# The shared expert's last two groups moved behind the routed rows

## The chip, the cores and the metric

The kernel runs on one core of one Trainium2 chip. The metric is the device time of one execution in microseconds (us). The core has five engines that run their own queues in order and meet at semaphores: PE (TensorE, matrix products into the PSUM banks), ACT (ScalarE), DVE (VectorE), POOL (GpSimd) and SP (SyncE, which issues DMA transfers). POOL issues DMA transfers too, among them scatters to rows named by an index, with or without an addition to what lies there.

## The reference, cut to what matters

Two transformer-like layers over 32 x 256 tokens of 128 features. The change works in the last part of the second layer. Its input `x` is normalised to `xn`, and `xn` once more, with learned weights, to `a`:

```
rh          = gelu(a @ res_inter_w + res_inter_b)          # the shared expert: every token
res_mlp_out = rh @ res_output_w + res_output_b
h           = gelu(dispatched @ inter_w[e] + inter_b[e])   # the routed experts: 8 of them, 1024 rows each
expert_out  = h @ output_w[e] + output_b[e]
moe_out     = each token's own expert row, times its gate
coef        = softmax(a @ res_coef)
out         = res_mlp_out * coef[:, :1] + moe_out * coef[:, 1:] + xn
final       = x + conv_part(xn) + out     # conv_part: long convolution, gated projection, normalisation
```

So the output of a token is a sum of the stream (`x + xn`), the convolution part, the shared expert and the routed expert.

## The kernel before, in words

The 8192 tokens are 64 tiles of 128, in 16 groups of four (`GROUPS = 16`, `GROUP = 4`). The function `shared_and_last` holds the whole last stage. Work of one group of 512 tokens on an expert is two steps on PE: `make_hidden` (`L1523`, four products of 512 columns, 128 hidden units each; on ACT `activate`, `L1695`, applies gelu) and `make_out` for the shared expert (`L1533`) or `make_tiles` for the routed ones (`L1550`), 16 products each. In float32 one product shows as two matmul rows.

The expert sequence counts `ALL = 32` groups: 0 to 15 are the shared expert over the tokens in order, 16 to 31 the routed rows, two groups for each of eight experts. A helper `half(i)` on each engine takes the steps in turn: odd `i` is a `make_hidden`, even `i` the output step of the group before. Halves 0 to 11 run beside the convolution. From half 12 they run in the loop over the gated projection, one in each round `g` and two in round 8.

A round `g` of that loop: PE turns four tiles (`turn_y`, `L1584`), takes its half, and projects (`project`, `L1592`). ACT applies gelu (`L1709`), the gate's tanh (`gate`, `L1714`) for group `g - 1`, its half, and normalises group `g - 2` (`normalise`, `L1723`). DVE scales group `g - 3` (`scale`, `L1914`), multiplies with the gate and measures group `g - 1` (`gate_and_measure`, `L1895` to `L1904`), takes its half (`evict`, `L1845` and `L1850`, which adds the shared expert's weighted output to the stream), forms an offset (`make_offset`, `L1909`) and adds the projection's bias (`add_bias`, `L1887`). POOL takes the root of group `g - 1` (`root`, `L1422`), adds the normalised group `g - 3` to the stream (`add`, `L1429`) and scatters three token tiles to their experts' rows in DRAM (`L1035`), until all 64 are out. `add(g)` waits for `scaled` and for `evicted`, so a finished group of the stream has all but its routed part. SP then stores it to the output (`store`, `L1371`).

After the loop come the routed rows. SP loads each group of rows (`load_rows`, `L1376`), PE turns it (`turn_rows`, `L1561`), DVE takes it (`take_rows`, `L1867` to `L1870`), PE and ACT make the hidden layer and the four tiles, DVE adds the bias and weighs the tile (`put_y`, `L1879` and `L1881`), and POOL scatters it with an addition to the output rows (`L1473`), one scatter for each of the 64 tiles, after a wait for all stores (`stored`). POOL ends with a wait for every scatter. The weights of experts 0 to 6 are loaded by `load_pack` (`L1380`) as soon as the last `turn_y` is done, since they lie where the projection's input lay. Those of expert 7 would lie over the shared expert's weights, so their load waits for the last shared `make_out`.

Of the kernel before, what the change touches and what calls it, by code (L numbers as in the profile page):

```python
# [17 lines left out]
ALU = mybir.AluOpType  # L18
# [3 lines left out]
P = 128  # L22
B, T, D = 32, 256, 128
# [1246 lines left out]
def shared_and_last(nc, a, m, out):  # L1270
# [16 lines left out]
    ALL = 2 * GROUPS  # L1287
    PER = GROUPS // E
    with ExitStack() as ctx:
        def sb(name, shape, dt=F32):  # L1290
# [54 lines left out]
                "y_turned", "yT_ready", "projected", "biased", "tanh", "gated", "stats", "raised", "rstd", "offset",  # L1345
                "normal", "scaled", "added", "scattered", "tile_downed", "tile_summed", "tile_ready")))
        tiles = lambda g: slice(g * GROUP, g * GROUP + GROUP)

        @block.sync
        def _(sp):  # L1350
# [28 lines left out]
            def load_pack(e):  # L1379
                sp.dma_start(m["packs"][:, e, :], a["experts1"][:, e, :]).then_inc(sem[f"pack{e}"], 16)  # L1380

# [22 lines left out]
        def _(pool):  # L1404
# [71 lines left out]
            for j in range(SENDS):  # L1476
                pool.wait_ge(sem[f"sent{j}"], 16 * GROUP * len(range(j, GROUPS, SENDS)))

        @block.tensor
        def _(pe):  # L1480
# [29 lines left out]

            def make_hidden(g, ks=range(KI)):
                r = g - GROUPS
                if r >= 0:
                    pe.wait_ge(sem["x_ready"], r + 1)
                    pe.wait_ge(sem[f"pack{r // PER}"], 16)
                    own, x = m["packs"][:, r // PER, :], xs[:, r % 2, :]
                else:
                    own, x = pack, xT[:, g * GN:g * GN + GN]
                for k in ks:
                    n = g * KI + k  # L1520
# [5 lines left out]
            def make_out(g):  # L1526
                pe.wait_ge(sem["hidden_ready"], (g + 1) * KI)
                if g:
                    pe.wait_ge(sem["summed"], g)
                for t in range(GROUP):  # L1530
                    for k in range(KI):
                        n = P_DOWN + D * k
                        ins = pe.matmul(ps[:, SHARED_OUT, P * t:P * t + P], hidden[:, g % 2, k, P * t:P * t + P],  # L1533
                                        pack[:, n:n + D], start=(k == 0), stop=(k == KI - 1))
                ins.then_inc(sem["downed"], 1)

            def make_tiles(r):
                g = GROUPS + r
                own = m["packs"][:, r // PER, :]
                pe.wait_ge(sem["hidden_ready"], (g + 1) * KI)  # L1540
                if r == 0:
                    pe.wait_ge(sem["summed"], GROUPS)
                for t in range(GROUP):
                    i = r * GROUP + t
                    if i >= len(TILE_OUT):
                        pe.wait_ge(sem["tile_summed"], i - len(TILE_OUT) + 1)
                    bank = ps[:, TILE_OUT[i % len(TILE_OUT)], 0:P]
                    for k in range(KI):
                        n = P_DOWN + D * k
                        ins = pe.matmul(bank, hidden[:, g % 2, k, P * t:P * t + P], own[:, n:n + D],  # L1550
                                        start=(k == 0), stop=(k == KI - 1))
                    ins.then_inc(sem["tile_downed"], 1)
# [12 lines left out]
            def half(i):  # L1565

                if i == 2 * ALL - 1:
                    make_tiles(GROUPS - 1)
                elif i % 2:
                    make_hidden((i + 1) // 2)  # L1570
                    if GROUPS <= (i + 1) // 2 + 1 < ALL:
                        turn_rows((i + 1) // 2 + 1 - GROUPS)
                elif i // 2 - 1 < GROUPS:
                    make_out(i // 2 - 1)
                else:
                    make_tiles(i // 2 - 1 - GROUPS)

# [100 lines left out]
        def _(act):  # L1678
# [6 lines left out]

            def activate(g):
                own = m["packs"][:, (g - GROUPS) // PER, :] if g >= GROUPS else pack
                if g >= 2:
                    act.wait_ge(sem["downed"], min(g - 1, GROUPS))
                    if g > GROUPS + 1:  # L1690
                        act.wait_ge(sem["tile_downed"], (g - 1 - GROUPS) * GROUP)
                for k in range(KI):
                    n = g * KI + k
                    act.wait_ge(sem["upped"], n + 1)
                    act.activation(hidden[:, g % 2, k, :], ps[:, n % 3, :], ACT.Gelu_apprx_tanh,  # L1695
                                   bias=own[:, P_BIAS + k:P_BIAS + k + 1]).then_inc(sem["hidden_ready"], 1)

            def half(i):

                if i % 2 and i < 2 * ALL - 1:  # L1700
                    activate((i + 1) // 2)
# [76 lines left out]
            for g in range(GROUPS):  # L1778
                take_yT(g)
                if g >= 1:  # L1780
                    gate(g - 1)
                half(done)
                done += 1
                if g >= 2:
                    normalise(g - 2)
                if g == 8:
                    half(done)
                    done += 1
            half(done)
            gate(GROUPS - 1)  # L1790
            normalise(GROUPS - 2)
            normalise(GROUPS - 1)
            for i in range(done + 1, 2 * ALL):
                half(i)

        @block.vector
        def _(dve):
# [43 lines left out]
            def evict(g):  # L1841
# [10 lines left out]
                ins.then_inc(sem["evicted"], 1)  # L1852

            def half(i):

                if i and i % 2 == 0:
                    evict(i // 2 - 1)

            def take_rows(r):
                dve.wait_ge(sem["rows_turned"], r + 1)  # L1860
                if r >= 2:
                    dve.wait_ge(sem["upped"], (GROUPS + r - 1) * KI)
                if r >= SENDS:
# [9 lines left out]
            def put_y(r):  # L1873
                own = m["packs"][:, r // PER, P_OUT:PACK]
# [119 lines left out]
            for g in range(GROUPS):  # L1994
                if g >= 3:
                    scale(g - 3)
                if g >= 1:
                    gate_and_measure(g - 1)
                half(done)
                done += 1  # L2000
                if g >= 1:
                    make_offset(g - 1)
                add_bias(g)
                if g == 8:
                    half(done)
                    done += 1
            scale(GROUPS - 3)
            take_rows(0)
            gate_and_measure(GROUPS - 1)
            make_offset(GROUPS - 1)  # L2010
            evict(GROUPS - 2)
            scale(GROUPS - 2)
            scale(GROUPS - 1)
            take_rows(1)
            evict(GROUPS - 1)
            for r in range(GROUPS):
                if r + 2 < GROUPS:
                    take_rows(r + 2)
                put_y(r)


# [73 lines left out]
```

## Time and profile before

| | us |
|---|---|
| median of 3 runs | 1256.83 |
| lowest and highest | 1256.32, 1257.4 |
| profiled execution | 1254.92 |
| its span | 1253.2 |

The page's busy times, as shares of the span:

| engine | busy us | share |
|---|---|---|
| PE matmul | 1130.6 | 90% |
| PE weight load | 814.1 | 65% |
| DVE | 889.6 | 71% |
| POOL | 734.2 | 59% |
| ACT | 648.8 | 52% |

The shares are means over the whole kernel. The change touches only the stretch from some 1050 us on, so that stretch is read by itself. In a row of the timeline the first number is the start, the second how long the instructions of the row lasted together, and a bracket gives the engine's idle time before it and what ended that. The chain's rows have start, duration, engine, tile and line.

### The profile page before, as it was taken

What the parts mean: (1) busy time and instruction counts of PE and PEld (TensorE: products, weight loads), DVE (VectorE), ACT (ScalarE), POOL (GpSimd) and SP (SyncE); (2) the same over time, 40 slices, a digit from 0 to 9 for tenths busy, and PEclk for the clock granted to TensorE, in tenths of its full rate; (3) what the DMA queues carried; (4) which work ended last, traced back from release to release, by engine and by line L of the source; (5) the groups of instructions that cost most, each with busy time, mean ns of one, the idle gap of its engine ahead of it and who ended that gap; (6) DMA issues with size and microseconds to landing.
All of it is one profiled execution on the core that took longest, in us unless ns stands there. A gap on an engine that the chain in (4) does not pass through costs nothing. (4 is left out here: it accounts for less than half of the span.)

```text
span 1253.2 us, 26697 instructions
## 1 busy us (share of the span) xinstructions
PE 1130.6 (90%) x9306; PEld 814.1 (65%) x9306; DVE 889.6 (71%) x2636; ACT 648.8 (52%) x1056; POOL 734.2 (59%) x908
## 2 busy tenths in 40 slices
PE   3963999999999969999999998999869899899994
PEld 2642555555555538999999896777646667667773
DVE  8986888888888746666666564888774489874442
ACT  4840777777777744444444344655523265553331
POOL 3204787777878754555555452334438567638886
PEclk9965999999999989999999998999889999999998
DMA  9904000000000012222222213122248312265543
GB/s 326 363 0 183 24 27 26 28 28 26 26 28 26 28 41 58 68 70 72 68 70 68 65 56 115 52 68 78 91 139 248 110 43 71 78 209 88 71 54 30
DMA packets 96813, 104.07 MB, mean 83 GB/s; under 512 B 12812, under 2 KB 84300, under 8 KB 96588
## 3 DMA queue, kind: packets, MB, share of 16 engines
q1 hardware_dynamic: 75792, 75.10, 19.5%
q0 software_dynamic: 19968, 26.63, 9.0%
q8 instruction: 61, 1.00, 0.3%
q10 hardware_dynamic: 956, 1.04, 0.3%
q14 instruction: 36, 0.29, 0.1%
HBM read 55.58 MB, written 47.15 MB: 82 GB/s over the span
## 5 line engine op out<-in xcount | busy, mean ns | idle before, releaser
L833 ACT ACTIVATE probs<-ps 128x1024 f32<-128x1024 f32 x256 | 254.5, 1025 | 110.2 <-PE ps L742 107.0
L1035 POOL DMA_INDIRECT slots<-rowbuf,slots x192 | 204.5, 1065 | 62.2 <-issue 36.3
L1146 POOL DMA_INDIRECT y<-slot_y,where x144 | 150.9, 1048 | 145.3 <-DVE slot_y L1127 121.7
L1214 ACT ACTIVATE slot_h<-ps,own 128x256 f32<-128x256 f32 x288 | 120.3, 470 | 153.7 <-PE ps L1178 152.0
L1178 PE MATMUL ps<-slot_x,own 128*128 128x256 f32 x576 | 141.1, 389 | 3.4 <-DVE slot_x L1116 2.9
L1190 PEld LDWEIGHTS ps<-own,slot_h 128*128 128x128 f32 x1152 | 140.4, 192 | 3.9 <-ACT slot_h L1214 0.2
L759 PE MATMUL ps<-probs,vext 128*32 128x256 f32 x2048 | 138.2, 388 | 3.1 <-issue 3.1
L1190 PE MATMUL ps<-own,slot_h 128*128 128x128 f32 x1152 | 140.6, 276 | 0.0
L1695 ACT ACTIVATE h<-ps,packs 128x512 f32<-128x512 f32 x128 | 85.5, 685 | 86.3 <-PE ps L1523 83.6
L1523 PE MATMUL ps<-xT,packs 128*128 128x512 f32 x256 | 119.1, 603 | 11.8 <-ACT h L1695 11.8
L1178 PEld LDWEIGHTS ps<-slot_x,own 128*128 128x128 f32 x576 | 105.2, 193 | 19.9 <-DVE slot_x L1116 8.0
L1473 POOL DMA_INDIRECT out<-xT,where x64 | 99.2, 1549 | 22.4 <-issue 12.8
L742 PE MATMUL ps<-q_stackT,k_stackT 32*128 32x256 f16 x1024 | 88.9, 276 | 6.0 <-ACT probs L833 2.7
L759 PEld LDWEIGHTS ps<-probs,vext 128*32 128x32 f32 x2048 | 53.7, 109 | 52.6 <-issue 23.6
L1441 POOL TENSOR_TENSOR roots_n<-spread_n,power 128x8 f32<-128x8 f32 x16 | 31.9, 1996 | 95.1 <-DVE spread_n L1964 95.1
L1523 PEld LDWEIGHTS ps<-xT,packs 128*128 128x128 f32 x256 | 45.9, 191 | 62.5 <-issue 42.2
L1091 DVE COPY own<-packs 128x1156 f32 x72 | 54.9, 763 | 39.9 <-issue 39.9
L742 PEld LDWEIGHTS ps<-q_stackT,k_stackT 32*128 32x128 f16 x1024 | 25.6, 92 | 73.8 <-issue 46.1
L1610 PE MATMUL ps<-pack,h 128*128 128x128 f32 x512 | 66.1, 291 | 3.3 <-ACTq L1748 3.3
L848 POOL TENSOR_TENSOR factor<-root 128x64 f32<-128x64 f32 x96 | 31.3, 326 | 64.2 <-DVEq L914 58.4
L1610 PEld LDWEIGHTS ps<-pack,h 128*128 128x128 f32 x512 | 63.6, 206 | 4.6 <-ACTq L1748 4.1
L1533 PE MATMUL ps<-packs,h 128*128 128x128 f32 x512 | 61.9, 280 | 4.7 <-DVE result L1845 4.7
(299 smaller groups left out, 2221.4 us busy)
## 6 DMA issues: line engine op xcount, KB each, us to landing
toeplitz<-conv_kernel SPq DMA_DIRECT2D x16, 1024.0 KB, 7.4
slots<-blank SPq DMA_DIRECT2D x26, 528.0 KB, 11.7
slot_rows<-slots SPq DMA_DIRECT2D x72, 132.0 KB, 2.2
routed<-y SPq DMA_DIRECT2D x32, 256.0 KB, 3.2
packs<-in_experts SPq DMA_DIRECT2D x1, 4624.0 KB, 14.5
packs<-in_experts SPq DMA_DIRECT2D x8, 578.0 KB, 6.8
xT<-slots SPq DMA_DIRECT2D x16, 264.0 KB, 2.8
stream<-in_x SPq DMA_DIRECT2D x8, 512.0 KB, 7.6
```

Of the source, the lines that this page charges most:

```text
L742: ins = pe.matmul(ps[:, 2 * (p % 2) + j, kt * T:kt * T + T], stackT[1][rows, b % 2, g, kt * P:kt * P + P], stackT[0][rows, b % 2, g, :], s ...
L759: ins = pe.matmul(ps[32 * r:32 * r + 32, PV[pair], 0:T], vext[:, first:first + VW], probs[:, (2 * g + r // 2) % 4, r % 2, kt, :], start=(k ...
L833: act.activation(probs[:, p % 4, :, :, :].rearrange("p j k t -> p j (k t)"), ps[:, 2 * (p % 2):2 * (p % 2) + 2, :], ACT.Exp, scale=DK ** - ...
L1035: return pool.indirect_dma_start(m["slot_dram"][layer], bass.IndirectOffsetOnAxis(ap=where, axis=0), m["rowbuf"][:, tile, :], None)
L1146: pool.indirect_dma_start(m["y_dram"][layer], bass.IndirectOffsetOnAxis(ap=where[:, j, h:h + 1], axis=0), y[:, j, h, :], None).then_inc(se ...
L1178: ins = pe.matmul(ps[:, 2 * (j % 2) + k // 2, (k % 2) * LOT:(k % 2) * LOT + LOT], own[:, j, P * k:P * k + P], xs[:, j % 2, :], start=True, ...
L1190: ins = pe.matmul(ps[:, 6 + j % 2, P * h:P * h + P], hidden[:, j % 2, k, P * h:P * h + P], own[:, j, n:n + D], start=(k == 0), stop=(k == ...
L1214: ins = act.activation(hidden[:, j % 2, k, :], ps[:, 2 * (j % 2) + k // 2, (k % 2) * LOT:(k % 2) * LOT + LOT], act_func, bias=own[:, j, P_ ...
L1473: pool.indirect_dma_start(out, bass.IndirectOffsetOnAxis(ap=where[:, r % SENDS, k:k + 1], axis=0), routed[:, r % SENDS, k, :], None, compu ...
L1523: pe.matmul(ps[:, n % 3, :], own[:, P * k:P * k + P], x, start=True, stop=True).then_inc(sem["upped"], 1)
L1610: ins = pe.matmul(ps[:, 4, P * t:P * t + P], hidden[:, g % 2, k, P * t:P * t + P], pack0[:, n:n + D], start=(k == 0), stop=(k == KI - 1))
L1695: act.activation(hidden[:, g % 2, k, :], ps[:, n % 3, :], ACT.Gelu_apprx_tanh, bias=own[:, P_BIAS + k:P_BIAS + k + 1]).then_inc(sem["hidde ...
```

## The change: what it does

The expert sequence is re-ordered (`ORDER`): shared groups 0 to 13, then the 16 routed groups, then shared groups 14 and 15. The halves stay one in each round for rounds 0 to 13, with no second half in round 8 and none in rounds 14 and 15. Shared outputs 12 and 13 (`make_out`, `evict`) come after the loop; so do both `turn_rows` that open the routed stage. The stream's groups 14 and 15 are stored without their shared part. At the end PE writes the two late shared groups to the banks that the turned rows used (`LATE_OUT`), DVE adds the bias and weighs them into a buffer (`evict_late`), and POOL, after all its scatters have landed, adds each of the two groups to the output by one direct transfer of 256 KB with an addition (`accum_op=ALU.add`). Expert 7's weights go to a buffer of the first layer (`pack0`) and are loaded with the other seven.

```diff
+    FIRST = GROUPS - 2
+    ORDER = list(range(FIRST)) + list(range(GROUPS, ALL)) + list(range(FIRST, GROUPS))
+    LATE_OUT = ROW_TURN
+    last_pack = lambda e: m["pack0"][:, :] if e == E - 1 else m["packs"][:, e, :]
...
-            for e in range(E - 1):
+            for e in range(E):
                 load_pack(e)
...
-            sp.wait_ge(sem["downed"], GROUPS)
-            load_pack(E - 1)
...
-                pool.wait_ge(sem["evicted"], g + 1)
+                pool.wait_ge(sem["evicted"], min(g + 1, FIRST))
...
             for j in range(SENDS):
                 pool.wait_ge(sem[f"sent{j}"], 16 * GROUP * len(range(j, GROUPS, SENDS)))
+            for g in range(FIRST, GROUPS):
+                pool.wait_ge(sem["late"], g - FIRST + 1)
+                pool.dma_start(final[:, tiles(g), :], z[:, g - FIRST, :, :], accum_op=ALU.add)\
+                    .then_inc(sem["late_added"], 16)
+            pool.wait_ge(sem["late_added"], 16 * (GROUPS - FIRST))
...
             for g in range(GROUPS):
                 turn_y(g)
-                half(done)
-                done += 1
-                project(g)
-                if g == 8:
+                if g < 14:
                     half(done)
                     done += 1
-            for i in range(done, 2 * ALL):
-                half(i)
+                project(g)
+            make_out(FIRST - 2)
+            turn_rows(0)
+            turn_rows(1)
+            make_out(FIRST - 1)
+            make_hidden(FIRST)
+            for i in range(FIRST + 1, ALL):
+                make_hidden(i)
+                r = i + 1 - FIRST
+                if r < GROUPS:
+                    turn_rows(r)
+                if i - 1 < FIRST + GROUPS:
+                    make_tiles(i - 1)
+                else:
+                    make_out(i - 1)
+            make_out(ALL - 1)
...
+            def evict_late(g):
+                dve.wait_ge(sem["downed"], g + 1)
+                some = z[:, g - FIRST, :, :]
+                if g == FIRST:
+                    dve.wait_ge(sem["added"], GROUPS)
+                tt(some, ps[:, LATE_OUT[g - FIRST], :].rearrange("p (k d) -> p k d", d=D),
+                   out1[:, :].unsqueeze(1).broadcast_to([P, GROUP, D]), ALU.add).then_inc(sem["summed"], 1)
+                dve.wait_ge(sem["summed"], g + 1)
+                tt(some, some, weights[:, tiles(g), E:E + 1].broadcast_to([P, GROUP, D]), ALU.mult)\
+                    .then_inc(sem["late"], 1)
...
             scale(GROUPS - 3)
+            evict(FIRST - 2)
             take_rows(0)
             gate_and_measure(GROUPS - 1)
+            take_rows(1)
             make_offset(GROUPS - 1)
-            evict(GROUPS - 2)
+            evict(FIRST - 1)
             scale(GROUPS - 2)
             scale(GROUPS - 1)
-            take_rows(1)
-            evict(GROUPS - 1)
             for r in range(GROUPS):
                 if r + 2 < GROUPS:
                     take_rows(r + 2)
                 put_y(r)
+            for g in range(FIRST, GROUPS):
+                evict_late(g)
```

## Rows read from the trace of the kernel before

**Rows 1.** The chain that ended last, its end: start us, us, engine, tile, line.

```profile
1221.60 0.44 PE ps L1561 x4
1222.04 3.57 PE ps L1550 x32
1225.61 3.44 PE ps L1523 x8
...
1244.70 1.55 POOL out L1473
```

**Rows 2.** The accumulating scatters of line 1473: durations, starts and landing.

```profile
L1473 POOL DMA_INDIRECT out<-xT,where x64: 1546/1546/1653, 1127.9 to 1244.7; - x64
...
DMA to landing us min/median/max: 3.2/3.3/4.8
```

**Rows 3.** The chain in the projection loop: POOL's roots 5, 7, 11, 12.

```profile
1039.19 1.04 POOL rstd L1422
...
1052.96 1.04 POOL rstd L1422
...
1081.86 1.04 POOL rstd L1422
...
1089.44 1.05 POOL rstd L1422
```

**Rows 4.** The timeline of the loop's last rounds: bias 13, 14, 15 and between.

```profile
1092.33 1.22 DVE L1887 TENSOR_TENSOR toeplitz<-ps,rows 128x1024 f32<-128x1024 f32 x1
...
1095.81 1.89 PE L1592 MATMUL ps<-w_out,toeplitz 128*128 128x256 f32 x8
...
1097.54 1.27 POOL L1429 TENSOR_TENSOR stream<-stream,toeplitz 128x512 f32<-128x512 f32 x1
1097.60 1.23 DVE L1909 TENSOR_TENSOR offset<-mv,rstd 128x4 f32<-128x4 f32 x1 [1.13 <-POOL rstd L1422]
...
1098.95 1.22 DVE L1887 TENSOR_TENSOR toeplitz<-ps,rows 128x1024 f32<-128x1024 f32 x1
...
1106.06 1.22 DVE L1887 TENSOR_TENSOR toeplitz<-ps,rows 128x1024 f32<-128x1024 f32 x1
```

**Rows 5.** The timeline from the loop's end to the routed rows, and PE's end.

```profile
1109.16 0.68 DVE L1895 SCALAR_TENSOR_TENSOR toeplitz<-toeplitz 128x512 f32<-128x512 f32 x1
...
1111.45 1.02 POOL L1422 TENSOR_TENSOR rstd<-rstd,power 128x4 f32<-128x4 f32 x1 [5.99 <-DVE rstd L1904]
...
1113.96 1.65 ACT L1723 ACTIVATE toeplitz<-toeplitz,offset,rstd 128x128 f32<-128x128 f32 x4 [4.30 <-DVE offset L1910]
...
1116.23 1.13 PE L1523 MATMUL ps<-xT,packs 128*128 128x512 f32 x2 [2.03 <-ACT h L1695]
...
1117.63 3.74 PE L1533 MATMUL ps<-packs,h 128*128 128x128 f32 x32
...
1121.41 0.69 DVE L1845 TENSOR_TENSOR result<-ps,out 128x512 f32<-128x512 f32 x1 [2.36 <-PE ps L1533]
...
1122.13 1.14 DVE L1850 SCALAR_TENSOR_TENSOR stream<-result,weights,stream 128x128 f32<-128x128 f32 x4
...
1125.08 3.74 PE L1550 MATMUL ps<-packs,h 128*128 128x128 f32 x32
...
1235.80 0.39 PE L1550 MATMUL ps<-packs,h 128*128 128x128 f32 x2
```

**Rows 6.** PE after an idle stretch: its timeline, then the slice with its granted clock.

```profile
937.30 5.44 PE L1533 MATMUL ps<-packs,h 128*128 128x128 f32 x32 [4.66 <-DVE result L1845]
...
938.00:939.00 1.00, 1.00 (x7) 1.00 (x6) 1.00 (x1) 0.00 (x0) 0.98 (x2) 0.50 0.96 304
```

**Rows 7.** A slice: PE, PEld, DVE, ACT, POOL busy; clock, DMA share, GB/s.

```profile
1104.00:1112.00 8.00, 7.45 (x45) 5.31 (x44) 6.98 (x23) 4.80 (x9) 2.01 (x3) 1.00 1.03 372
```

**Rows 8.** DMA from 1110 on: queue packets, MB, share; issues, KB, landing.

```profile
q0 software_dynamic: 9216, 4.20, 32.4%
...
out<-stream SPq DMA_DIRECT2D x3, 256.0 KB, 2.4
```

More of the change, by code:

```diff
@@ L1345, in shared_and_last @@
                 "y_turned", "yT_ready", "projected", "biased", "tanh", "gated", "stats", "raised", "rstd", "offset",
-                "normal", "scaled", "added", "scattered", "tile_downed", "tile_summed", "tile_ready")))
+                "normal", "scaled", "added", "scattered", "tile_downed", "tile_summed", "tile_ready", "late", "late_added")))
         tiles = lambda g: slice(g * GROUP, g * GROUP + GROUP)
@@ L1379, in load_pack @@
             def load_pack(e):
-                sp.dma_start(m["packs"][:, e, :], a["experts1"][:, e, :]).then_inc(sem[f"pack{e}"], 16)
+                sp.dma_start(last_pack(e), a["experts1"][:, e, :]).then_inc(sem[f"pack{e}"], 16)
             for g in range(GROUPS - 6):
@@ L1509, in turn, with make_hidden @@
                 ins.then_inc(sem["turned"], 1)
-            def make_hidden(g, ks=range(KI)):
+            def make_hidden(i, ks=range(KI)):
+                g = ORDER[i]
                 r = g - GROUPS
@@ L1515, in make_hidden @@
                     pe.wait_ge(sem[f"pack{r // PER}"], 16)
-                    own, x = m["packs"][:, r // PER, :], xs[:, r % 2, :]
+                    own, x = last_pack(r // PER), xs[:, r % 2, :]
                 else:
@@ L1519, in make_hidden @@
                 for k in ks:
-                    n = g * KI + k
+                    n = i * KI + k
                     if n >= 3:
@@ L1524, in make_hidden, with make_out @@
                               start=True, stop=True).then_inc(sem["upped"], 1)
-            def make_out(g):
-                pe.wait_ge(sem["hidden_ready"], (g + 1) * KI)
-                if g:
+            def make_out(i):
+                g = ORDER[i]
+                pe.wait_ge(sem["hidden_ready"], (i + 1) * KI)
+                if g >= FIRST:
+                    pe.wait_ge(sem["x_ready"], GROUPS)
+                elif g:
                     pe.wait_ge(sem["summed"], g)
+                bank = LATE_OUT[g - FIRST] if g >= FIRST else SHARED_OUT
                 for t in range(GROUP):
@@ L1532, in make_out, with make_tiles @@
                         n = P_DOWN + D * k
-                        ins = pe.matmul(ps[:, SHARED_OUT, P * t:P * t + P], hidden[:, g % 2, k, P * t:P * t + P],
+                        ins = pe.matmul(ps[:, bank, P * t:P * t + P], hidden[:, i % 2, k, P * t:P * t + P],
                                         pack[:, n:n + D], start=(k == 0), stop=(k == KI - 1))
                 ins.then_inc(sem["downed"], 1)
[L1537 to L1540, printed above, removed]
+            def make_tiles(i):
+                r = ORDER[i] - GROUPS
+                own = last_pack(r // PER)
+                pe.wait_ge(sem["hidden_ready"], (i + 1) * KI)
                 if r == 0:
-                    pe.wait_ge(sem["summed"], GROUPS)
+                    pe.wait_ge(sem["summed"], FIRST)
                 for t in range(GROUP):
[L1544 to L1547, printed above, removed]
+                    n = r * GROUP + t
+                    if n >= len(TILE_OUT):
+                        pe.wait_ge(sem["tile_summed"], n - len(TILE_OUT) + 1)
+                    bank = ps[:, TILE_OUT[n % len(TILE_OUT)], 0:P]
                     for k in range(KI):
-                        n = P_DOWN + D * k
-                        ins = pe.matmul(bank, hidden[:, g % 2, k, P * t:P * t + P], own[:, n:n + D],
+                        first = P_DOWN + D * k
+                        ins = pe.matmul(bank, hidden[:, i % 2, k, P * t:P * t + P], own[:, first:first + D],
                                         start=(k == 0), stop=(k == KI - 1))
@@ L1565, in half @@
             def half(i):
-                if i == 2 * ALL - 1:
-                    make_tiles(GROUPS - 1)
-                elif i % 2:
+                if i % 2:
                     make_hidden((i + 1) // 2)
-                    if GROUPS <= (i + 1) // 2 + 1 < ALL:
-                        turn_rows((i + 1) // 2 + 1 - GROUPS)
-                elif i // 2 - 1 < GROUPS:
+                else:
                     make_out(i // 2 - 1)
-                else:
-                    make_tiles(i // 2 - 1 - GROUPS)
             def turn_y(g):
@@ L1667, in _ @@
                 turn_y(g)
-                half(done)
-                done += 1
-                project(g)
-                if g == 8:
+                if g < 14:
                     half(done)
                     done += 1
-            for i in range(done, 2 * ALL):
-                half(i)
+                project(g)
[11 more added lines that the diff above has]
+                    make_tiles(i - 1)
+                else:
+                    make_out(i - 1)
+            make_out(ALL - 1)
         @block.scalar
@@ L1684, in take_chunk, with activate @@
                    .then_inc(sem["yb_ready"], 1)
[L1686 to L1691, printed above, removed]
+            def activate(i):
+                g = ORDER[i]
+                own = last_pack((g - GROUPS) // PER) if g >= GROUPS else pack
+                if i >= 2:
+                    before = ORDER[i - 2]
+                    if before >= GROUPS:
+                        act.wait_ge(sem["tile_downed"], (before - GROUPS + 1) * GROUP)
+                    else:
+                        act.wait_ge(sem["downed"], before + 1)
                 for k in range(KI):
-                    n = g * KI + k
+                    n = i * KI + k
                     act.wait_ge(sem["upped"], n + 1)
-                    act.activation(hidden[:, g % 2, k, :], ps[:, n % 3, :], ACT.Gelu_apprx_tanh,
+                    act.activation(hidden[:, i % 2, k, :], ps[:, n % 3, :], ACT.Gelu_apprx_tanh,
                                    bias=own[:, P_BIAS + k:P_BIAS + k + 1]).then_inc(sem["hidden_ready"], 1)
             def half(i):
-                if i % 2 and i < 2 * ALL - 1:
+                if i % 2:
                     activate((i + 1) // 2)
@@ L1781, in _ @@
                     gate(g - 1)
-                half(done)
-                done += 1
+                if g < 14:
+                    half(done)
+                    done += 1
                 if g >= 2:
                     normalise(g - 2)
[L1786 to L1789, printed above, removed]
             gate(GROUPS - 1)
@@ L1792, in _ @@
             normalise(GROUPS - 1)
-            for i in range(done + 1, 2 * ALL):
-                half(i)
+            for i in range(FIRST, ALL):
+                activate(i)
         @block.vector
@@ L1873, in put_y @@
             def put_y(r):
-                own = m["packs"][:, r // PER, P_OUT:PACK]
+                own = last_pack(r // PER)[:, P_OUT:PACK]
                 for k in range(GROUP):
@@ L1998, in _ @@
                     gate_and_measure(g - 1)
-                half(done)
-                done += 1
+                if g < 14:
+                    half(done)
+                    done += 1
                 if g >= 1:
```

5 lines of the change are left out of this document (1 added, 4 removed).

## The prediction

> **What bounds the kernel now.** I read the granted clock and the slices first, then the chain that ended last, from its end backwards, then the timeline of the 60 us in which the change works. The reader is to see three things.
>
> First, the end. The chain closes with PE's last matmuls and then only POOL's accumulating scatters [rows 1]. They start at 1127.9 and 1244.7 and there are 64 [rows 2], so one goes out every 116.8 / 63 = 1.85 us, 7.41 for the four of a group. PE's period for a routed group is 3.57 + 3.44 + 0.44 = 7.45 [rows 1]. The two are nearly equal; POOL ends with a backlog because it starts late and because PE's last group has no hidden matmuls behind it. The last scatter starts at 1244.7 and lands after 3.3 [rows 2], at 1248.0; the span ends at 1253.2, so 5.2 us lie behind the last landing, and I keep them.
>
> Second, the start of the routed stage: PE's first routed output matmuls at S = 1125.08 [rows 5]. PE ends at 1236.2 [rows 5], that is S + 111.1: 16 outputs, 14 hidden and 13 turns give 57.1 + 48.2 + 5.7 = 111.0 by the pieces above. The span ends at S + 128.1.
>
> Third, what holds S up. In the loop over the gated projection POOL is the bound: root (`L1422`), add and three scatters make 13.77 us per two groups (1039.19 to 1052.96 [rows 3]), until its scatters are out at 1089.4. From there it is the chain bias, gate, measure, root, offset, bias: 6.62 from 1092.33 to 1098.95 [rows 4]. Behind the loop group 15 must still be measured and normalised before ScalarE may activate the first routed rows [rows 5].
>
> **What the change removes ahead of S.** PE loses two hidden and two output steps of the shared expert, 2 x (3.44 + 3.57) = 14.0 us, but PE isn't what is late there, so I follow the chain.
>
> *The loop.* The double half at g = 8 goes. Root(7) is at 1052.96 and root(11) at 1081.86 [rows 3]; two beats after 1052.96 would be 1080.50. So 1.4 come back. POOL's last four scatters put root(12) 7.58 behind root(11) (1081.86 to 1089.44 [rows 3]), now 1088.1. Bias 13 then waits for the root (1.04), a POOL add (1.27) that held the small VectorE offset for 1.23 instead of letting it run [rows 4], and no eviction: 2.5 behind the root, 1090.6 instead of 1092.33. Bias 14 is 6.62 later, 1097.2. Bias 15 is some 5.5 later, since POOL's add(12) now stands waiting for evict(12) and holds nobody: 1102.7, done at 1103.9, against 1106.06 + 1.22 = 1107.3 before. So the loop ends 3.4 earlier.
>
> *What takes this back.* Evict(12) (0.69 + 1.14 [rows 5]) now stands in VectorE's queue ahead of the first rows and of measure 15. It needs make_out(12), which is now behind project(15). And PE has only the turns and a projection of 1.89 [rows 4] in each of the last two rounds, of some 6 us. After the one idle of 4.66 in the rows, PE took 5.44 for 32 matmuls that otherwise take 3.74 [rows 5, 6], at a granted clock of 0.50, that is 1.2 GHz [rows 6]: 1.7 lost. I charge that once: project(15) from 1098.5 to 1102.1, make_out(12) to 1105.7, evict(12) to 1107.6. POOL's add(12) is then let go and holds VectorE for 1.25, the rows take 1.2 (of the 1.88 from 1107.28 to 1109.16, less a scale of 0.68), and measure 15 its 2.29 (1109.16 to 1111.45 [rows 5]): root(15) at 1112.3, where it stood at 1111.45. From root to normalise it was 2.51; without the add's hold, but with the second rows taken ahead of the offset, 1.5: normalise 15 at 1113.8 instead of 1113.96. Without the slow clock it would be 1113.0. Behind the waiting add(12) stand root(15) and the adds and stores 13 to 15; evict(13) ends 1.9 behind the offset at 1115.7, three adds of 1.27 at 1119.5, and the last store lands 2.4 later [rows 8], at about 1122, in time for POOL's first scatter.
>
> *From there to S.* Before, 11.12 from 1113.96 to 1125.08 [rows 5]. Of it one output step and one turn go, 3.57 + 0.44 = 4.0; make_out(13) and the turns now lie beside VectorE's chain. S' = 1113.8 + 7.1 = 1120.9, 4.2 earlier. Bounds: a second slow stretch while PE waits for normalise 15 (it waited 2.03 there before [rows 5]; now longer) gives +1.7, so -2.5; the loop's whole 3.4 kept gives -4.0 - 3.4 = -7.4.
>
> *The queues.* SP issues pack 7 with the other seven and no longer waits for the last shared output; the stage in which these load holds 372 GB/s [rows 7], so its 578 KB delay the stores by 1.6. Those are wanted only at 1122. If they were late, POOL's start would move by that 1.6, less the 10 us by which PE now ends later than POOL: nothing.
>
> **What it adds behind the routed rows.** PE: 14.0, so PE ends at S' + 111.1 + 14.0 = S' + 125.1. VectorE's evict_late: two operations of 128 x 512 at 0.69, with starts 1.6: late(15) at S' + 126.7. POOL: its 64 scatters started 2.8 behind S; now the last starts near S' + 2.3 + 116.8 = 119.1 and has landed at 122.4. The first transfer waits for late(14): PE ends that at S' + 121.5, late at 123.1. So it goes out at 123.4 and hides under PE's last output if its issue is under 3.6 us. The second goes out at S' + 127.0, and all of it is on the path: nothing stands behind it but the end.
>
> Its price isn't in the trace: no direct transfer is issued by POOL. From below, SP's store of the same 256 KB: 2.4 [rows 8]. From above, four accumulating scatters of 64 KB in place of one transfer: 3 x 1.85 + 3.3 = 8.9 [rows 2]. The nearest row is the scatter: same queue, same addition, a quarter of the rows, 3.3. From 1110 on q0 moved 9216 packets in 32.4% of 16 engines' 143.2 us [rows 8], 0.081 us a packet and engine; 384 more rows over 16 engines are 24 x 0.081 = 1.9. I take 5.2.
>
> The Trainium skill's DMA: Bandwidth & Descriptors (Anatomy of one DMA) fits a POOL-issued transfer with about 2.0 us plus its bytes at 436 GB/s; by that the transfer would be 2.6 and the time 1259.3, near rival A below. The trace speaks against it: the same formula makes 2.15 of the scatter that took 3.3.
>
> **The sum.** New span: S' + 127.0 + 5.2 + 5.2 = S' + 137.4 = 1258.3, against 1253.2: +5.1. The profiled execution took 1254.92, so 1260.0 by its own time; the runs' median lies 1.9 above that, 1256.83, so I predict 1261.9.
>
> **The rivals.**
>
> *A, a cheap transfer.* It lands in 2.4, as the store does, and all else holds: 5.1 - 2.8 = +2.3, 1259.1. For it: the store of the same bytes. Against: an accumulating scatter of a quarter takes longer already.
>
> *B, the issue grows with the rows.* POOL would need four times 1.55 = 6.2 for each transfer [rows 2]. The first, out at 123.4, ends at 129.6, the second at 136.1, and lands 1.75 later (3.3 - 1.55): S' + 137.9, the end at S' + 143.1, +10.8, 1267.6. For it: one scatter of 128 rows does take 1.55. Against: a direct transfer reads no indices.
>
> *C, PE is the bound ahead of S.* If the whole 14.0 came off the path there, S' = S - 14.0; with +9.3 behind, -4.7: 1252.1. The place is PE's queue between g = 8 and the first routed output. It decides for faster once S' is more than 11.8 earlier. For it: PE is busy 7.45 of 8 from 1104 on [rows 7]. Against: PE still waited 2.03 for ScalarE at 1116.23, and the chain runs over POOL [rows 3, 5].
>
> **How the numbers follow.** About 0.2%, 2.5 us, is what a measurement can tell from no change. The forecast has 0.60 with its own range of 1259.3 to 1265 (S' by its bounds, the transfer 4 to 7); A 0.15, B 0.13, C 0.12. From 1258 to 1268 only C and the tails are left out, some 0.16. Faster is C, 0.12; A and the forecast's lowest part are within 0.2%, 0.18; the rest, 0.70, is slower.
>
> **What would show it.** Right: first routed output near 1121, loop done near 1104 but root(15) no earlier than 1111; PE's last matmul some 125 behind the first routed output; the chain ending in PE, VectorE and POOL's second direct transfer, not in scatters. Wrong: a first routed output before 1114 (C); a transfer's issue of over 3.6 us (B); from the last issue to the landing under 3 (A); or scatters that still end last.

## The result, and the profile after

The changed kernel takes 1261.35 us (median of 8 runs, 1260.56 to 1263.68) against 1256.63 (8 runs, 1255.52 to 1258.4) on the same chip: ratio 1.0038, interval [1.0028, 1.0048], so 3.5 to 6.0 us slower. The prediction was 1261.9. The profiled execution took 1261.27 with a span of 1259.5.

The timeline from bias add 14 to the first routed output shows the gain of the loop and where it is lost (start us, us, engine, line, operation; in brackets the idle time ahead and its releaser). It answers to [rows 4, 5].

```profile
1097.37 1.23 DVE L1915 TENSOR_TENSOR toeplitz<-ps,rows 128x1024 f32<-128x1024 f32 x1
...
1098.74 3.75 PE L1598 MATMUL ps<-w_out,toeplitz 128*128 128x256 f32 x8 [4.21 <-DVE toeplitz L1915]
...
1102.28 4.52 PE L1545 MATMUL ps<-packs,h 128*128 128x128 f32 x32
...
1102.91 1.23 DVE L1915 TENSOR_TENSOR toeplitz<-ps,rows 128x1024 f32<-128x1024 f32 x1
...
1106.84 0.69 DVE L1862 TENSOR_TENSOR result<-ps,out 128x512 f32<-128x512 f32 x1 [2.10 <-PE ps L1545]
...
1108.89 1.25 DVE L1897 TENSOR_SCALAR where<-place 128x4 int32<-128x4 f32 x1
...
1113.06 1.02 POOL L1424 TENSOR_TENSOR rstd<-rstd,power 128x4 f32<-128x4 f32 x1 [2.94 <-DVE rstd L1932]
...
1114.51 1.65 ACT L1743 ACTIVATE toeplitz<-toeplitz,offset,rstd 128x128 f32<-128x128 f32 x4 [8.16 <-DVE offset L1938]
...
1116.78 6.26 PE L1531 MATMUL ps<-xT,packs 128*128 128x512 f32 x10 [2.71 <-ACT h L1715]
...
1123.31 3.74 PE L1562 MATMUL ps<-packs,h 128*128 128x128 f32 x32
```

The last bias add starts at 1102.91 instead of 1106.06, so 3.2 earlier; the first routed output at 1123.31 instead of 1125.08, only 1.8 earlier. Group 15 is normalised at 1114.51, no earlier than the 1113.96 of before: there the loop's gain is gone, and the 1.8 come from the shorter way behind it, 8.8 instead of 11.1. PE's two idle stretches, 4.21 and 2.71, are each followed by matmuls that are too long: 3.75 for a projection of 1.89 [rows 4], 6.26 for ten matmuls of 128 x 512. The slices show why (from:to, length, busy time of PE, PEld, DVE, ACT and POOL, then the granted clock, DMA share, GB/s): the clock stands at 0.50, which is 1.2 GHz, and is back at 2.4 GHz only at 1121.

```profile
1098.00:1099.00 1.00, 0.26 (x1) 0.29 (x2) 1.00 (x2) 0.37 (x1) 0.00 (x0) 0.50 1.00 412
...
1118.00:1119.00 1.00, 1.00 (x3) 0.48 (x2) 0.00 (x0) 0.69 (x1) 1.00 (x2) 0.50 0.00 0
1119.00:1120.00 1.00, 1.00 (x2) 0.43 (x2) 0.00 (x0) 0.09 (x1) 1.00 (x2) 0.50 0.48 135
...
1121.00:1122.00 1.00, 1.00 (x3) 0.38 (x2) 0.00 (x0) 0.65 (x1) 0.02 (x1) 1.00 0.97 323
```

The chain that ended last answers to [rows 1]: PE's late output matmuls, VectorE's add and weight, POOL's second transfer. ("Issue" is time in which the engine waited for nothing that the profile shows.)

```profile
1237.85 3.44 PE ps L1531 x8
1241.29 7.16 PE ps L1545 x64
1248.45 0.02 issue
1248.47 0.70 DVE toeplitz L1876
1249.17 0.02 issue
1249.20 0.70 DVE toeplitz L1879
1249.90 0.28 issue
1250.18 1.28 POOL out L1482
```

The queries of the two POOL lines give the price that was not in the trace before, and what answers to [rows 2]. The scatters are what they were; the last starts 7.2 ahead of the second transfer's issue.

```profile
L1482 POOL DMA_DIRECT2D out<-toeplitz x2: 1283/1324/1366, 1247.0 to 1250.2; - x2
...
DMA to landing us min/median/max: 4.3/4.5/4.7
...
L1475 POOL DMA_INDIRECT out<-xT,where x64: 1544/1551/1639, 1126.0 to 1243.0; - x64
```

The first of the two landings is the 4.7, the second the 4.3: the same query over the time from 1249 on holds the second transfer alone and gives 4.3. So it lands at 1250.18 + 4.3 = 1254.5, and the span ends at 1259.5: 5.0 lie behind it.

### The profile page after: what moved, and what is told of

It is laid out like the page before. It is cut to its first block and busy times, and to the rows that moved or that the text cites. A ratio compares the mean times of both kernels' runs of the same rounds, so it can differ in the third digit from the quotient of the medians.

```text
span 1259.5 us, 26692 instructions
## 1 busy us (share of the span) xinstructions
PE 1134.5 (90%) x9306; PEld 814.4 (65%) x9306; DVE 885.7 (70%) x2630; ACT 650.7 (52%) x1056; POOL 740.3 (59%) x910
## 3 DMA queue, kind: packets, MB, share of 16 engines
q1 hardware_dynamic: 75792, 75.10, 19.3%
## 5 line engine op out<-in xcount | busy, mean ns | idle before, releaser
L1035 POOL DMA_INDIRECT slots<-rowbuf,slots x192 | 207.9, 1083 | 62.0 <-issue 37.9
L1531 PE MATMUL ps<-xT,packs 128*128 128x512 f32 x240 | 115.3, 620 | 13.0 <-ACT h L1715 13.0
L1715 ACT ACTIVATE h<-ps,packs 128x512 f32<-128x512 f32 x120 | 80.1, 685 | 78.9 <-PE ps L1531 76.5
L1616 PE MATMUL ps<-pack,h 128*128 128x128 f32 x512 | 62.7, 282 | 3.4 <-ACTq L1768 3.3
L1545 PEld LDWEIGHTS ps<-packs,h 128*128 128x128 f32 x512 | 60.9, 198 | 5.6 <-issue 5.5
```

Source lines behind the costliest of these rows:

```text
L1035: return pool.indirect_dma_start(m["slot_dram"][layer], bass.IndirectOffsetOnAxis(ap=where, axis=0), m["rowbuf"][:, tile, :], None)
L1531: pe.matmul(ps[:, n % 3, :], own[:, P * k:P * k + P], x, start=True, stop=True).then_inc(sem["upped"], 1)
L1545: ins = pe.matmul(ps[:, bank, P * t:P * t + P], hidden[:, i % 2, k, P * t:P * t + P], pack[:, n:n + D], start=(k == 0), stop=(k == KI - 1))
L1715: act.activation(hidden[:, i % 2, k, :], ps[:, n % 3, :], ACT.Gelu_apprx_tanh, bias=own[:, P_BIAS + k:P_BIAS + k + 1]).then_inc(sem["hidde ...
```

## The experiments

Every kernel was timed in five rounds. Single executions reach the projection loop up to 8 us apart, whatever the kernel, so their spans can't be compared directly. I cut each profiled span at three starts: bias add 0, bias add 15, the first routed output. "Whole" is from bias add 0 to the end of the span; the ratio is that of the timed runs to the kernel before.

| kernel | bias 0 at | to bias 15 | to first routed output | to the end | whole | ratio |
|---|---|---|---|---|---|---|
| before | 1002.9 | 103.2 | 19.0 | 128.1 | 250.3 | 1 |
| after | 1002.7 | 100.2 | 20.4 | 136.2 | 256.8 | 1.0038 [1.0028, 1.0048] |
| e1, no transfers | 1003.7 | 99.9 | 19.1 | 128.1 | 247.0 | 0.9968 [0.9954, 0.9982] |
| e2, front only | 1003.8 | 99.9 | 19.2 | 128.1 | 247.1 | 0.9965 [0.9952, 0.9979] |
| e3, PE kept busy | 1004.2 | 99.9 | 16.6 | 137.1 | 253.5 | 1.0024 [1.0013, 1.0035] |
| e4, measure first | 1004.9 | 100.2 | 16.8 | 136.5 | 253.5 | 1.0020 [1.0007, 1.0032] |
| e5, before + pack | 998.6 | 103.0 | 19.0 | 128.1 | 250.2 | 0.9998 [0.9987, 1.0008] |
| e6, before reordered | 1005.9 | 103.2 | 17.0 | 128.1 | 248.2 | 0.9994 [0.9979, 1.0009] |
| e7, SP stores | 1003.1 | 99.8 | 19.3 | 130.1 | 249.3 | 1.0004 [0.9993, 1.0014] |
| e8, e6 once more | 1004.8 | 103.2 | 17.0 | 128.1 | 248.3 | 0.9991 [0.9977, 1.0004] |
| e9, e3 and e4 | 998.1 | 99.8 | 20.1 | 136.4 | 256.3 | 1.0053 [1.0040, 1.0066] |

Up to the first routed output e1, e2 and e7 run the code of the changed kernel, yet they have 19.1 to 19.3 where it has 20.4. The rows of e1 show the difference (they answer to the changed kernel's projection of 3.75, output of 4.52 and hidden products of 6.26):

```profile
1099.35 3.41 PE L1593 MATMUL ps<-w_out,toeplitz 128*128 128x256 f32 x8 [4.21 <-DVE toeplitz L1910]
...
1102.59 3.73 PE L1540 MATMUL ps<-packs,h 128*128 128x128 f32 x32
...
1116.31 6.05 PE L1526 MATMUL ps<-xT,packs 128*128 128x512 f32 x10 [2.72 <-ACT h L1710]
```

Both slow stretches are there, but the output of group 12 runs at its usual speed in e1, e2 and e7 (3.73 in each). So some 1.2 us of the changed kernel's 20.4 belong to its one traced execution, and its whole of 256.8 is high by as much.

**The changed kernel without its two transfers.**

```diff
-            for g in range(FIRST, GROUPS):
-                pool.wait_ge(sem["late"], g - FIRST + 1)
-                pool.dma_start(final[:, tiles(g), :], z[:, g - FIRST, :, :], accum_op=ALU.add)...
-            pool.wait_ge(sem["late_added"], 16 * (GROUPS - FIRST))
```

> The changed kernel without its two accumulating transfers at the end (the late groups' shared part is computed but doesn't reach the output). Theory: the second transfer stands alone on the path, 4.3 to 4.7 us from its start to its landing in the changed kernel's profile, so the time falls by about 4.5, from 1261.4 to 1256.9, and PE's last outputs and VectorE's late(15) end the chain. Rival, POOL's scatters set the end and the transfers only follow them: they have landed at 1246.3, so about 8 less, 1253. Rival, the late PE work alone costs it all and the transfer is hidden: no change, 1261.

Measured: 1253.0 against 1256.68, ratio 0.9968 [0.9954, 0.9982]. Beside the 1.0038 of the changed kernel that is 0.0070, 8.8 us. The theory's 4.5 is missed, and the first rival's 8 came out: without the transfers the scatters set the end. The end of its chain of waits shows VectorE's last piece ending at 1249.2; its scatters' query and the span (the query's first line) show what really ends it.

```profile
1240.61 7.16 PE ps L1540 x64
...
1248.52 0.69 DVE toeplitz L1874
```

```profile
core 0 of [0], span 1250.7 us
...
L1475 POOL DMA_INDIRECT out<-xT,where x64: 1546/1546/1654, 1125.6 to 1242.4; - x64
```

The last scatter lands at 1242.4 + 3.3 = 1245.7 and the span ends 5.0 later, as before (5.2). From the first routed output it takes 128.1, as it did before. So PE's late work costs nothing by itself: PE ends it at 1247.8 and VectorE at 1249.2, both inside the 5.0 behind the last scatter's landing. All that the changed kernel loses at its end hangs on the transfers: of the 8.1 (136.2 for 128.1), 7.3 are the later start of the last DMA, which must wait for that late work (126.9 behind the first routed output, where the last scatter stood at 119.6), and most of the rest is its longer landing (4.3 for 3.3).

**The late groups left out altogether.** PE, ScalarE, VectorE and POOL drop their last-two-groups code; the front keeps its new order.

```diff
-            make_out(ALL - 1)
+            make_tiles(FIRST + GROUPS - 1)
...
-            for i in range(FIRST, ALL):
+            for i in range(FIRST, FIRST + GROUPS):
                 activate(i)
```

> The changed kernel's front alone: shared groups 14 and 15 are left out of the work altogether, on PE, ScalarE, VectorE and POOL. Theory: the first scatter starts at 1126.0 where it started at 1127.9, and the end is POOL's again, so 1.9 under the kernel before, 1254.7, although PE does 14.0 us less. Rival, the front is bound by PE and the changed kernel's late end hides the gain: 7 to 14 less than before, 1243 to 1250.

Measured: 1252.85, 0.9965 [0.9952, 0.9979]: 2.6 to 6.0 us under before, more than the theory's 1.9 and less than the rival's 7. The table has 3.2, all of it in the loop (103.2 to 99.9); from bias add 15 to the first routed output it gains nothing (19.2). It equals the kernel without transfers, which says again that the late matmuls are free.

**PE kept busy in its idle stretches.** Matmuls into free banks that nobody reads:

```diff
+                if g == GROUPS - 1:
+                    pe.wait_ge(sem["summed"], FIRST - 2)
+                    fill(SHARED_OUT, 4)
                 project(g)
...
-            make_hidden(FIRST)
+            make_hidden(FIRST, range(3))
+            fill(7, 3)
+            make_hidden(FIRST, range(3, KI))
```

> The changed kernel with matmuls that nobody reads in PE's two idle stretches: four products of 512 columns ahead of project(15), three ahead of the first routed group's last hidden product. Theory: both stretches of 1.2 GHz behind them go; make_out(12) ends 2.0 earlier, so evict(12), root(15) and normalise 15 do, and the hidden products that took 6.26 take 1.8 less: 3.8 less than the changed kernel, 1257.6, first routed output near 1119.5, granted clock 1.00 from 1098 to 1123. Rival, the queue order on VectorE holds the chain and the clock costs nothing: no change, 1261.4. Rival, the extra products delay PE: up to 3 more.

Measured: 1259.47 (9 runs) against 1256.68, 1.0024 [1.0013, 1.0035]. The timeline, from bias add 14 on, for the rows that were slow in the changed kernel:

```profile
1098.52 1.22 DVE L1924 TENSOR_TENSOR toeplitz<-ps,rows 128x1024 f32<-128x1024 f32 x1
1099.89 1.97 PE L1602 MATMUL ps<-w_out,toeplitz 128*128 128x256 f32 x8 [0.77 <-DVE toeplitz L1924]
...
1101.69 3.73 PE L1545 MATMUL ps<-packs,h 128*128 128x128 f32 x32
...
1115.83 4.53 PE L1531 MATMUL ps<-xT,packs 128*128 128x512 f32 x10 [0.23 <-ACT h L1724]
```

With more matmuls in the queue the same work is done sooner: projection 1.97 instead of 3.75, output 3.73 instead of 4.52, hidden 4.53 instead of 6.26. From bias add 15 to the first routed output it is 16.6 instead of 20.4, or of the 19.1 to 19.3 that the same code took in three other traces. So the slow stretches do stand in the way at the front. Some of it comes back at the end (137.1 instead of 136.2), where the two transfers now go out 1.3 apart and take 4.4 and 5.2 to land. By the ratios the fill is worth 0.0014, 1.8 us, where 3.8 were expected; the two ratios come from different sets of runs and their intervals overlap, so the times alone don't show a gain.

**The measure of group 15 first.** VectorE measures group 15 ahead of evict(12) and the first rows; POOL takes its root ahead of add(12), and the eviction of group 13 goes ahead of the second rows.

```diff
-                if g >= 3:
+                if g >= 3 and g != GROUPS - 1:
+                    if g == GROUPS:
+                        add(GROUPS - 4)
                     add(g - 3)
...
+            gate_and_measure(GROUPS - 1)
             evict(FIRST - 2)
+            make_offset(GROUPS - 1)
             take_rows(0)
-            gate_and_measure(GROUPS - 1)
+            evict(FIRST - 1)
             take_rows(1)
-            make_offset(GROUPS - 1)
-            evict(FIRST - 1)
```

> The changed kernel with another order behind the loop: on VectorE measure 15 ahead of evict(12) and of the rows, on POOL root(15) ahead of add(12). No work is added or left out. Theory: the place of evict(12) ahead of measure 15 is what ate the loop's gain; measure 15 starts at 1104.8 instead of 1110.8, the wait is then on PE and the rows, first routed output near 1119 instead of 1123.3: 4.4 less than the changed kernel, 1257. Rival, PE's queue is the bound ahead of the routed rows: within 1 of 1261.4.

Measured: 1259.57 against 1256.68, 1.0020 [1.0007, 1.0032]. Bias add 15 to root(15) is now 4.2 instead of 10.15, and 16.8 to the first routed output. By the ratios it is worth 2.3 us, where 4.4 were expected, and here too the intervals overlap. The cost is a new wait: the eviction stands behind the measure, and PE waits for it.

```profile
1105.11 1.22 DVE L1917 TENSOR_TENSOR toeplitz<-ps,rows 128x1024 f32<-128x1024 f32 x1
...
1109.16 0.69 DVE L1864 TENSOR_TENSOR result<-ps,out 128x512 f32<-128x512 f32 x1
1109.33 1.01 POOL L1424 TENSOR_TENSOR rstd<-rstd,power 128x4 f32<-128x4 f32 x1 [4.53 <-DVE rstd L1934]
...
1110.00 3.81 PE L1547 MATMUL ps<-packs,h 128*128 128x128 f32 x32 [0.97 <-DVE result L1864]
```

**Both edits together.**

> The changed kernel with both edits that were tried alone: matmuls whose results nobody reads in PE's two idle stretches (e3_fill: 16.56 us from bias add 15 to the first routed output instead of 20.40) and the measure of group 15 first on VectorE with its root first on POOL (e4_measure_first: 16.77). Theory (the idle stretch and the slow clock behind it are two halves of one chain, so the gains don't add; PE's own work behind bias add 15 is 14.0: 1.3 rest of the output of group 12, 1.1 turns, 3.8 output of group 13, two hiddens of 3.6, 0.6 turns): 14 to 15.5, some 1.5 us below either, median 1257.5 to 1258, ratio 1.0005. Rival (the gains add): 12.9, below PE's own work, which would show a part of that work moved ahead of bias add 15; median 1256, ratio 0.9995. Rival (the two edits remove the same wait): 16.6, median 1259.5, ratio 1.002. In all of them first routed output to the end of the span is 136 to 137, as with the transfers at the end.

Measured: 1261.15 (6 runs) against 1254.04, 1.0053 [1.0040, 1.0066]: no better than the changed kernel, and all three expectations missed, 20.1 instead of 12.9 to 16.6. In the profiled execution, the shortest of the six (1256.14), the output of group 13 starts 4.89 behind bias add 15, to the hundredth as in measure first alone, since VectorE's measure and eviction set it. PE only stands ready earlier, waits 2.21 instead of 0.97, and is slow behind that wait (the timeline, then the slice with its granted clock):

```profile
1097.94 1.22 DVE L1926 TENSOR_TENSOR toeplitz<-ps,rows 128x1024 f32<-128x1024 f32 x1
...
1101.99 0.69 DVE L1873 TENSOR_TENSOR result<-ps,out 128x512 f32<-128x512 f32 x1
...
1102.83 5.44 PE L1547 MATMUL ps<-packs,h 128*128 128x128 f32 x32 [2.21 <-DVE result L1873]
...
1110.69 2.74 PE L1588 MATMUL ps<-xT,packs 128*128 128x512 f32 x6
```

```profile
1104.00:1106.00 2.00, 2.00 (x12) 2.00 (x11) 1.16 (x5) 0.30 (x1) 1.30 (x1) 0.50 1.05 340
```

The slow output (5.44 for 3.81) makes 1.6 of the 3.3 by which the stretch is over that of measure first alone. The other 1.7 lie behind it: the three products that nobody reads (`L1588`, 2.74) stand on PE's path there, where measure first alone had a wait of 0.67. The expectation's 14.0 for PE's own work had left them out. Whether the other five executions look the same no trace shows; their times fit the whole of 256.3, which is 6.0 over before's.

**The kernel before with the moved pack alone.**

```diff
-            for e in range(E - 1):
+            for e in range(E):
                 load_pack(e)
...
-            sp.wait_ge(sem["downed"], GROUPS)
-            load_pack(E - 1)
```

> The kernel before with one part of the change alone: expert 7's weights go to the first layer's buffer and load with the other seven. Theory: no one waits for them at either place (the first product with them is 100 us later), so within 0.2% of the kernel before, 1254.2 to 1259.2. Rival, the load that stood beside the last store (issued 0.4 behind it) held POOL's first scatter: 0.5 to 1 less, with the first scatter at 1127.0 to 1127.4 rather than 1127.9.

Measured: 1256.61 against 1257.24, 0.9998 [0.9987, 1.0008], and no stretch of the table moves by over 0.2. The pack's place is not the cause.

**SP stores the late groups.** Plain stores in place of POOL's accumulating transfers; SP waits for the scatters first. The stores replace the rows, so this kernel leaves out all but the shared part of the two groups.

```diff
+            for g in range(FIRST, GROUPS):
+                sp.wait_ge(sem["late"], g - FIRST + 1)
+                sp.dma_start(final[:, tiles(g), :], z[:, g - FIRST, :, :])...
```

> The changed kernel with its two late groups written by two plain stores on SP, at the same place behind all scatters, in place of the two accumulating transfers on POOL (the store replaces the rows instead of adding to them). Theory: some 5.0 lie between the last landing and the span's end only where POOL issued the last transfer (kernel before, changed kernel, front alone), while leaving the transfers out gave 8.8, the 4.5 of the transfer and most of that 5.0. A store that goes out at late(15), lands 2.4 later and has 1.5 behind it ends 5.6 sooner than the changed kernel: 1255.8. Rival, the 5.0 follow any last landing: only the 2.1 between the two landings are saved, 1259.3.

Measured: 1256.84 against 1257.24, 1.0004 [0.9993, 1.0014]; 0.0034 under the changed kernel, 4.3 us, and 6.1 in the profile's last stretch (130.1 for 136.2). Between the two expectations, nearer the larger. The query of the store's line, with the span:

```profile
core 0 of [0], span 1252.4 us
...
L1408 SPq DMA_DIRECT2D out<-toeplitz x2: 388/388/389, 1245.5 to 1248.9; - x2
...
DMA to landing us min/median/max: 2.3/2.3/2.3
```

Its last store lands at 1251.2, and the span ends 1.2 later (the expectation's 1.5 stood in no trace). So the 5 us don't lie behind whatever lands last; they go with POOL's last DMA, or with POOL's queue being the last to end, which no run tells apart. The expectation had put much of what the kernel without transfers saved down to this stretch; but that kernel has its 5.0 too, behind its last scatter. Here the last scatter starts at 1241.9 and lands at 1245.2, and 5.0 behind that is 1250.2, ahead of the store's landing.

**The kernel before with the measure of group 15 ahead of the first rows.**

```diff
-            take_rows(0)
             gate_and_measure(GROUPS - 1)
+            take_rows(0)
...
                 pool.wait_ge(sem["evicted"], g + 1)
+                if g == GROUPS - 3:
+                    pool.wait_ge(sem["offset"], GROUPS)
```

> The kernel before with two orders changed behind the loop and nothing moved to the end: VectorE measures group 15 ahead of taking the first rows, and POOL's add(13) waits until the offset is formed. Theory: the chain from bias 15 over measure, root, offset and normalise 15 sets the start of the routed stage; it gets 1.1 (the rows) and 1.1 (the add's hold) shorter, PE then has no idle ahead of it, and nothing is added at the end: 2.2 less, 1254.4, first routed output near 1122.8. Rival, PE's queue is already the bound there: within 0.5 of 1256.7.

> The kernel before with VectorE's measure of group 15 ahead of taking the first routed rows and POOL's add of group 13 behind the last offset, the same edit as in e6_before_reordered, timed once more, since its time was unclear. Theory (the end of the loop is a chain through VectorE and POOL, and the 2.1 us that its profile showed between the last bias add and the first routed output, 16.95 instead of 19.02, reach the end): median 2 us under the kernel before, ratio 0.9983, and again about 17.0 from bias add 15 to the first routed output. Rival (what is gained there is lost in the arrival of the loop's end, bias add 15 from bias add 0 longer than 103.2): ratio 1.000.

Measured: 1255.13 against 1257.24, 0.9994 [0.9979, 1.0009], and 1253.97 against 1254.04, 0.9991 [0.9977, 1.0004]. In both profiles the stretch is 2.1 shorter, as expected. PE has no idle stretch of a microsecond in it and its hidden matmuls follow at full speed:

```profile
1109.09 1.22 DVE L1889 TENSOR_TENSOR toeplitz<-ps,rows 128x1024 f32<-128x1024 f32 x1
...
1113.47 1.02 POOL L1422 TENSOR_TENSOR rstd<-rstd,power 128x4 f32<-128x4 f32 x1 [4.98 <-DVE rstd L1906]
1113.57 0.17 DVE L1871 TENSOR_SCALAR where<-place 128x4 int32<-128x4 f32 x1
...
1114.50 3.82 PE L1525 MATMUL ps<-xT,packs 128*128 128x512 f32 x8
```

Its `where` takes 0.17 here, with POOL's add out of its way, and 1.25 in the changed kernel. The times show about half, and both intervals hold 1.000 as well as the theory's 0.9983. Whether this version beats the kernel before stays open; of the versions that leave nothing out, none is shown faster than the kernel before.

## Why the prediction was right

The forecast's mechanism held, and no rival did. Its point was 0.55 above the measured median, but that is partly luck, since two errors cancelled (see *The sum*).

*The loop, right.* Bias adds 14 and 15 were forecast at 1097.2 and 1102.7; they came at 1097.37 and 1102.91. The front-only kernel confirms the gain of some 3 us in what is measured from bias add 0.

*The take-back, right in place.* Project(15) ran at 1.2 GHz from 1098.74 (forecast 1098.5), evict(12) ended at 1108.7 (1107.6), POOL's add held VectorE for 1.25, root(15) came at 1113.06 (1112.3), and normalise 15 at 1114.51 (1113.8): nothing of the loop's gain was left there.

*From there to the first routed output, wrong.* The term was S' = 1113.8 + 7.1 = 1120.9; it was 1123.31. The second slow stretch stood in the prediction only as a bound, +1.7. It came: PE waited 2.71 where it had waited 2.03, and the ten hidden matmuls behind it took 6.26. In the kernel that fills the wait (0.23 left) they took 4.53, 1.7 less. The other 0.7 came down from make_out(12), which was also partly slow in the traced execution. The second slow stretch is in e1, e2 and e7 too (6.05 to 6.12 for the ten, behind waits of 2.72 or 2.73), so the bound would have been the better value.

*PE's late work, right.* Late(15) was forecast at S' + 126.7, the second issue at S' + 127.0; it came at 126.87. PE's last matmul was forecast 125.1 behind the first routed output and ended there. What the prediction did not say is that this work alone costs nothing: it counted the way to the end as one sum, and the kernel without transfers showed that PE's and VectorE's part is hidden under the scatters and the 5.0 behind their landing. Its price appears only when a transfer waits for it.

*The transfer, mechanism right, a little too dear.* 5.2 was taken; the transfer on the path took 4.3 and the other 4.7, between the store's 2.4 and the 8.9 of four scatters. The nearest row, the scatter's 3.3, was the right guide, but the 1.9 for its further rows was about twice too much. The Trainium skill's DMA: Bandwidth & Descriptors (Anatomy of one DMA) made 2.6 of it; the measurement decides against that for an accumulating transfer. The issue took 1.28 to 1.37 and not 6.2, so rival B is out: it doesn't grow like four scatters.

*The stretch behind the last landing, right by luck.* I kept 5.2 without knowing whose it was; it was 5.0, with POOL again the last to issue. Had the stores gone by SP, it would have been 1.2.

*The sum.* S' was 2.4 too early; the issue, landing and tail were 0.1, 0.9 and 0.2 too dear. That gives +1.2 on the profiled span: 1259.5 instead of 1258.3. Against it stands the 1.9 that was added from the profiled execution to the median: it was 0.1 here (1261.27 and 1261.35). The timed runs show 4.7 between the medians, less than the profiled 6.5 of the table; some 1.2 of that difference is the traced execution's longer first slow stretch, which e1, e2 and e7 don't have. The measured time lies in the stated range, but the range's lower end of 1259.3 doesn't follow from the bounds named beside it: with S' 7.4 ahead of S instead of 4.2, and a transfer of 4, they reach 1257.5.

*Rival C* asked for a first routed output before 1114; it needed PE as the bound ahead of it, and PE idled for 4.21 and 2.71. Of its 14.0 some 3 came off the path, by the front-only kernel. *Rival A* asked for a landing under 3. Even then the order would hardly have won: the kernel with SP's landing of 2.3 and a tail of 1.2 is only level with before.

## What to carry to other kernels

Ask of work that is put behind the last stage which engine it extends: matmuls there can be free under the backlog of another queue, while a DMA that has to wait for them moves the last landing, and whatever stands between that and the end moves with it. Taking work from an engine that isn't the bound makes holes in its queue, and a hole can halve TensorE's clock for the work behind it, so put a price on every hole of a few us that ends on the path, not on the first alone. Compare profiled spans only after cutting them at events that both kernels share; the start of a stage can differ by more than the change.

## What the runs showed of the hardware

- Behind the last landing of a DMA that POOL issued, 5.0 to 5.2 us passed to the end of the span (in all ten traces where such a DMA landed last); behind SP's last store 1.2. What happens in it, the profile doesn't show.
- An accumulating direct transfer of 256 KB from POOL: issue 1.28 to 1.37, landing 4.3 to 4.7 (up to 5.2 where two went out 1.3 apart); SP's plain store of the same tiles 2.3. Whether the addition or the issuing engine makes the difference, no run tells.
- PE's waits of 2.71 (changed kernel) and 2.21 (both edits) were followed by stretches at the granted clock 0.50, which is 1.2 GHz, while one of 0.97 (measure first) was followed by matmuls at their usual 3.81. The wait alone doesn't settle it: in the kernel without transfers PE waited 2.71 ahead of the projection of group 14 too, and that ran in 1.97.
- A POOL tensor operation of 1.27 held a 128 x 4 VectorE operation to 1.25 instead of 0.17 where the two met in the changed kernel; in the reordered kernel before, where they don't meet, it takes 0.17. The Trainium skill's SBUF — State Buffer (SBUF: two separate sides) tells of a port pair that one of the two engines holds for a whole instruction; the trace agrees, since the small operation ends with POOL's (1108.85 + 1.27 beside 1108.89 + 1.25).
